# Time mixing: the bonus added by VectorE ahead of one centring product, in place of a second centring product

## The chip, the cores and the metric

The kernel runs on one core of one Trainium2 chip. The metric is the time of one execution on the device in microseconds (us); the figure of a kernel is the median of its runs. The kernel before was run three times: 3210.70, 3211.75 and 3214.01 us, median 3211.75 us.

## What is computed

The reference is one RWKV-like layer (time mixing, then channel mixing) followed by two cross attentions and an MLP. Only the end of time mixing matters here. Per batch and head (32 heads of size S = 16, 128 time steps):

```python
def step(s, rkvw):
    r_t, k_t, v_t, w_t = rkvw
    a = k_t[:, :, :, None] * v_t[:, :, None, :]
    out = jnp.einsum('bhk,bhkd->bhd', r_t, u * a + s)
    return (a + w_t[:, :, :, None] * s, out)
...
a4 = att.reshape(b, l, H, S)
m = jnp.mean(a4, axis=-1, keepdims=True)
var = jnp.mean((a4 - m) ** 2, axis=-1, keepdims=True)
att = ((a4 - m) * jax.lax.rsqrt(var + EPS)).reshape(b, l, E) * gn_w + gn_b
x = x + att * g @ Wo.T
```

`out` is a sum of two parts: what the state gives (`r_t` on `s`) and the bonus (`r_t` on `u * a`, which is `v_t` times the head's sum of `u * r_t * k_t`). The group norm then takes off each head's mean. Taking off the mean is linear: it can be done on the two parts one by one and added, or on their sum.

## The kernel before

Time mixing (`time_mix`, the first 890 us of the execution) works on the 16 batches in four quads (`q`) of four batches. A tile is 128 channels (8 heads) by 512 columns (4 batches of 128 time steps), and there are four channel groups (`f` or `g`, 0 to 3).

For each quad `body` first makes the projections, and then runs the recurrence in 32 steps `t`. Group g = t // 8 takes eight steps, and a step serves two of the 16 value positions of each head. In a step:

- TensorE: `spread(t + 2)`, four matmuls (lines 763 and 764) that spread values over a head's channels into two banks of `vb`; then `accumulate(t - 1)`, two fp32 matmuls (line 683) that sum the products of an earlier step into `mx[g % 2]`. An fp32 matmul stands in the trace as two passes.
- ScalarE: writes the initial state into `vb` (line 452), after `spread`.
- VectorE: a product with the keys (line 581), then two scans over time (line 586) with the result in `state`.
- GpSimd: the product of the state and the receptance (line 308).

`spread(T)` waits until VectorE has ended the scans of step T - 2. `accumulate` waits for GpSimd.

The group norm of group f is laid over the steps after it, at places written by hand: at t = 8f + 10 `attended` (ScalarE, line 352) copies the finished sum from `mx[f % 2]` into `h5`, and `centred` (TensorE, lines 689 and 690) multiplies it by the matrix `centre`, and adds the product of `centre` and the bonus, which GpSimd has left in `vv` (line 272). At 8f + 12 come `square` (ScalarE) and `variance` (TensorE, line 699), at 8f + 14 `deviation` (ScalarE, line 364), `inverse` (VectorE, line 549) and `unpacks` (TensorE, line 705), at 8f + 15 `gated` (VectorE, lines 554 and 558, it waits for `unpacks`). `gate` (TensorE, six matmuls at t = 8f + 3 and 8f + 5) and `bonus` (TensorE line 749, ScalarE line 424 at the next step) lie between them. Thus for f = 0 and 1 all of it falls into the recurrence. For f = 2 `attended` and `inverse` do, and `gated` comes after it. All of group 3's comes after it.

Between two quads stands `joint`: the output product (line 710), the end of the group norm of groups 2 and 3, and the start of the next quad: `norm_stats` and `norm_apply` (VectorE, lines 507 to 519; the latter writes `xf`, which the products of steps 28 and 29 also used), `transposes` (TensorE, line 658, it waits for all four tiles of `norm_apply`), `normalised` (ScalarE, line 333), `shift` (VectorE, lines 523 to 532) and `lora` (TensorE, line 664, each waits for its tile of `shift`). After the last quad stands `closing`, with no next quad to start. Each engine executes its own list in order. `joint` of VectorE before is:

```python
norm_stats(q + 1)
gated(q, 2)
v.wait_ge(rs_used, q * STEPS + (STEPS - 2))
norm_apply(q + 1)
v.wait_ge(rs_ready, q * STEPS + STEPS)
v.wait_ge(rs_used, q * STEPS + STEPS)
shift(q + 1)
```

`rs_used` counts the `accumulate`s.

Of the kernel before, what the change touches and what calls it, by code (L numbers as in the profile page):

```python
# [19 lines left out]
ALU = mybir.AluOpType  # L20
ACT = mybir.ActivationFunctionType
# [5 lines left out]
B, L, E = 16, 128, 512  # L27
# [58 lines left out]
def time_mix(nc, io, x2):  # L86
    J = 6
    MIX = [None, 1, 2, 3, 0, 4]
    STEPS = 32
    with ExitStack() as ctx:  # L90
# [18 lines left out]
        centre = sb("centre", [P, P])  # L109
# [67 lines left out]
        def quad3(ap):  # L177
            return ap.rearrange("p (b t) -> p b t", b=4)
# [60 lines left out]
        @block.gpsimd  # L239
        def _(gp):  # L240
            gp.memset(eps[:], EPS).then_inc(ready, 1)
            gp.memset(rest[:], 0.0).then_inc(x2_out, 16)

            def pack(s, m):
                hi, lo = (h5_split[32 * m:32 * m + 32, 0, :], h5_split[32 * m:32 * m + 32, 1, :]) if m < 4 else (
                    h5_split[0:LORA, 2, :], h5_split[0:LORA, 3, :])
                for k, part in enumerate((hi, hi, lo)):
                    gp.dma_start(packed[32 * k:32 * k + 32, s, :], part).then_inc(pack_in[min(s, 1)], 16)

            def lo(q, j, c):  # L250
                gp.wait_ge(hi_ready, q * 16 + (4 * j - 8 + c + 1))
                gp.tensor_tensor(x_lo[:, c, :], xf[:, c, :], x_hi[:, c, :], ALU.subtract).then_inc(split_ready, 1)

            def value_lo(q, c):
                if q == 0 and c == 0:
                    gp.wait_ge(w_ready, 4)
                gp.wait_ge(v_hi_ready, q * 4 + (c + 1))
                gp.tensor_tensor(quad3(v_lo[:, c, :]), vv[:, c, :, 0:L], quad3(v_hi[:, c, :]), ALU.subtract).then_inc(v_split_ready, 1)

            def receptance_key(q, f):  # L260
                gp.wait_ge(f_free, q * 12 + (8 + f + 1))
                if f == 0:
                    gp.wait_ge(decay_full, q * 4 + 4)
                else:
                    gp.wait_ge(bonus_full, q * 4 + f)
                if f >= 2:
                    gp.wait_ge(cent_full, q * 4 + (f - 1))
                gp.tensor_tensor(quad3(h5[:]), quad3(rr[:, f, :]), kk[:, f, :, 1:L + 1], ALU.mult).then_inc(rk_ready, 1)

            def bonus(q, f):  # L270
                gp.wait_ge(bonus_out, q * 4 + (f + 1))
                gp.tensor_tensor(vv[:, f, :, 1:L + 1], quad3(ew[:]), vv[:, f, :, 1:L + 1], ALU.mult).then_inc(bonus_used, 1)

            gp.wait_ge(w_ready, 2)
            gp.memset(wd[:], 0.0).then_inc(ready, 1)
            for q in range(NQ):
                gp.wait_ge(hl_hi, q * 2 + 1)
                gp.tensor_tensor(h5_split[:, 1, :], h5[:], h5_split[:, 0, :], ALU.subtract).then_inc(hl_lo, 1)
                gp.wait_ge(hl_lo, q * 2 + 1)
                for s in range(3):  # L280
                    pack(s, MIX[s + 2])
                gp.wait_ge(hl_hi, q * 2 + 2)
                gp.tensor_tensor(h5_split[0:LORA, 3, :], h4, h5_split[0:LORA, 2, :], ALU.subtract).then_inc(hl_lo, 1)
                gp.wait_ge(hl_lo, q * 2 + 2)
                pack(3, MIX[5])
                for j in range(2, 5):
                    for c in range(3):
                        lo(q, j, c)
                        if j == 4:
                            value_lo(q, c)  # L290
                    if j == 4:
                        value_lo(q, 3)
                    lo(q, j, 3)
                    if q == 0 and j == 2:
                        gp.wait_ge(w_hi_ready, 4)
                        gp.memset(vv[:, :, :, 0:1], 0.0).then_inc(pad_ready, 1)
                gp.wait_ge(mx_full, q * 20 + 20)
                gp.memset(kk[:, :, :, 0:1], 1.0).then_inc(pad_ready, 1)
                for c in range(EC):
                    lo(q, 5, c)  # L300
                gp.wait_ge(split_ready, q * 16 + 16)
                receptance_key(q, 0)
                for t in range(STEPS):
                    if t >= 4:
                        gp.wait_ge(rs_used, q * STEPS + (t - 3))
                    gp.wait_ge(scanned, q * (3 * STEPS) + 3 * (t + 1))
                    g = t // 8
                    gp.tensor_tensor(prod[t % 4], state[t % 2], rr[:, g:g + 1, :].broadcast_to([P, 2, QT]), ALU.mult).then_inc(rs_ready, 1)
                    for f in range(EC):
                        if t == 8 * f - 2:  # L310
                            receptance_key(q, f)
                        if t == 8 * f + 1:
                            bonus(q, f)

        @block.scalar
        def _(act):
# [20 lines left out]
            def hi(q, j, c, first=False):  # L337
# [6 lines left out]
                elif not first:  # L344
                    act.wait_ge(g_full, q * 4)
                act.activation(x_hi[:, c, :], xf[:, c, :], ACT.Copy).then_inc(hi_ready, 1)

            def attended(q, f):
                act.wait_ge(rs_used, q * STEPS + 8 * (f + 1))
                if f < 3:  # L350
                    act.wait_ge(bonus_full, q * 4 + (f + 2))
                act.activation(h5[:], mx[f % 2][:], ACT.Copy).then_inc(att_ready, 1)

            def square(q, f):
                act.wait_ge(cent_full, q * 4 + (f + 1))
# [35 lines left out]
            def body(q, first):  # L391
# [57 lines left out]
                for t in range(STEPS):  # L449
                    act.wait_ge(vb_full, q * STEPS + (t + 1))  # L450
                    d = 2 * (t % 8)
                    act.activation(vb[:, 2 * (t % 2):2 * (t % 2) + 2, 0:QT:L], s0[:, t // 8, d:d + 2, :], ACT.Copy).then_inc(s0_set, 1)  # L452
                    for f in range(EC):
                        if t == 8 * f + 1:
                            bonus(f)
                        if t == 8 * f + 7:
                            gate(f)
                        if t == 8 * f + 10:
                            attended(q, f)
                        if t == 8 * f + 12:  # L460
                            square(q, f)
                        if t == 8 * f + 14:
                            deviation(q, f)

            def joint(q):
                roots(q + 1)
                attended(q, 3)
                act.wait_ge(rs_ready, q * STEPS + STEPS)
                for c in range(EC):
                    normalised(q + 1, c)  # L470
                square(q, 3)
                deviation(q, 3)
                front(q + 1, False)

            def closing(q):
                attended(q, 3)
                square(q, 3)
                deviation(q, 3)

# [16 lines left out]
        def _(v):  # L496
# [38 lines left out]
            def mix(q, j):  # L535
                for c in range(EC):
# [7 lines left out]
                    v.wait_ge(mx_scaled, q * 20 + (n + 1))  # L544
                    v.tensor_tensor(quad3(xf[:, c, :]), quad3(mx[n % 2][:]), xn[:, c, :, 1:L + 1], ALU.add).then_inc(xf_ready, 1)

            def inverse(q, f):
                v.wait_ge(gstd_ready, q * 4 + (f + 1))
                v.reciprocal(grs[:], grs[:]).then_inc(grstd_ready, 1)
# [17 lines left out]
            def body(q, first):  # L567
# [6 lines left out]
                for t in range(STEPS):  # L574
# [10 lines left out]
                    for d in range(2):  # L585
                        v.tensor_tensor_scan(state[t % 2][:, d, :], wd[:, g].rearrange("p b t -> p (b t)"), pair[:, d, :], 0.0,  # L586
                                             ALU.mult, ALU.add).then_inc(scanned, 1)
                    for f in range(3):
                        if t == 8 * f + 14:
                            inverse(q, f)  # L590
                        if t == 8 * f + 15 and f < 2:
                            gated(q, f)

            def joint(q):
                norm_stats(q + 1)
                gated(q, 2)
                v.wait_ge(rs_used, q * STEPS + (STEPS - 2))
                norm_apply(q + 1)
                v.wait_ge(rs_ready, q * STEPS + STEPS)
                v.wait_ge(rs_used, q * STEPS + STEPS)  # L600
                shift(q + 1)
                inverse(q, 3)
                gated(q, 3)
                mix(q + 1, 1)
                mix(q + 1, 2)
                residual(q)

            def closing(q):
                gated(q, 2)
                inverse(q, 3)  # L610
                gated(q, 3)
                residual(q)
# [25 lines left out]
        def _(pe):  # L638
# [46 lines left out]

            def centred(q, f):
                pe.wait_ge(att_ready, q * 4 + (f + 1))
                pe.wait_ge(bonus_used, q * 4 + (f + 1))
                pe.matmul(mx[f % 2][:], centre[:], h5[:], start=True, stop=False)
                pe.matmul(mx[f % 2][:], centre[:], vv[:, f, :, 1:L + 1], start=False, stop=True).then_inc(cent_full, 1)  # L690

            def variance(q, f):
                if f < 3:
# [1403 lines left out]
```

## Time and profile before

| | |
|---|---|
| median of three runs | 3211.75 us |
| the profiled execution | 3213.54 us |
| its span, as the trace has it | 3211.7 us |
| TensorE busy | 3041.9 us, 95% |
| VectorE busy | 1812.5 us, 56% |
| ScalarE busy | 1195.8 us, 37% |
| GpSimd busy | 571.4 us, 18% |
| mean granted TensorE clock | 0.977 of full speed |

The 1.8 us between the span and the execution's time lie around the program. The busy shares are means over stages that differ a lot. The change touches time mixing alone, where GpSimd is busy too and VectorE is much busier than in the rest, so the shares of the whole say little on it. The stretches of the recurrence are about 108 to 238, 320 to 446, 530 to 654 and 740 to 868 us; the three joints follow the first three, the closing the last.

### The profile page before, as it was taken

What the parts mean: (1) busy time and instruction counts of PE and PEld (TensorE: products, weight loads), DVE (VectorE), ACT (ScalarE), POOL (GpSimd) and SP (SyncE); (2) the same over time, 40 slices, a digit from 0 to 9 for tenths busy, and PEclk for the clock granted to TensorE, in tenths of its full rate; (3) what the DMA queues carried; (4) which work ended last, traced back from release to release, by engine and by line L of the source; (5) the groups of instructions that cost most, each with busy time, mean ns of one, the idle gap of its engine ahead of it and who ended that gap; (6) DMA issues with size and microseconds to landing.
All of it is one profiled execution on the core that took longest, in us unless ns stands there. A gap on an engine that the chain in (4) does not pass through costs nothing.

```text
span 3211.7 us, 41965 instructions
## 1 busy us (share of the span) xinstructions
PE 3041.9 (95%) x15168; PEld 2387.6 (74%) x15168; DVE 1812.5 (56%) x2654; ACT 1195.8 (37%) x2584; POOL 571.4 (18%) x391
## 2 busy tenths in 40 slices
PE   6889899898969799999999999999999999999899
PEld 3545446455457688888888887878888888888787
DVE  5785986868767444445544446455444454444644
ACT  3224123232244343433443434334343454343432
POOL 2664655646500100000100001000000010000100
PEclk8999999999989899999999999999999999999999
DMA  4001000010032411111111111121111111111011
GB/s 131 17 10 38 7 17 31 7 41 1 0 117 82 163 53 36 52 36 53 37 38 51 40 48 35 64 73 46 52 36 52 36 53 36 52 36 42 27 46 59
DMA packets 54178, 148.64 MB, mean 46 GB/s; under 512 B 5936, under 2 KB 7472, under 8 KB 52848
## 3 DMA queue, kind: packets, MB, share of 16 engines
q1 hardware_dynamic: 51792, 144.45, 13.1%
q0 software_dynamic: 2304, 3.15, 0.5%
q8 instruction: 46, 0.75, 0.1%
q14 instruction: 36, 0.29, 0.0%
HBM read 131.85 MB, written 12.58 MB: 45 GB/s over the span
## 4 chain that ended last, share of the span: by engine, by line
PE 64%; DVE 2%; ACT 1%; issue 0%; DMA 0%; ACTq 0%; DVEq 0%
PE ca_ps L60 18%; PE ca_ps L62 18%; PE ca_ps L61 18%; PE ca_ps L1874 4%; PE ca_ps L1858 4%; PE ca_ps L1866 2%; PE ca_ps L1900 0%; DVE ca_stats L68 0%; DVE ca_xres L1635 0%; DMA ca_xres<-in_ctxT 0%; DVE ca_wq_lo L1593 0%; ACT ca_sk L1551 0%; DVE ca_ctx_lo L1666 0%; DVE ca_h_lo L1660 0%; ACT L1551 0%
## 5 line engine op out<-in xcount | busy, mean ns | idle before, releaser
L1635 DVE TENSOR_TENSOR ca_xres<-ca_xres,ca_ps 128x512 f32<-128x512 f32 x384 | 264.1, 688 | 243.9 <-PE ca_ps L62 238.9
L1422 ACT ACTIVATE ca_pr<-ca_ps,ca_nb 128x129 f32<-128x129 f32 x512 | 181.8, 368 | 511.9 <-DVE ca_nb L1618 511.9
L60 PE MATMUL ca_ps<-ca_h_hi,ca_wq_hi 128*128 128x512 f32 x768 | 313.3, 408 | 3.8 <-DVE ca_h_lo L1660 3.3
L586 DVE TENSOR_TENSOR_SCAN tm_xn<-tm_wd,tm_vb 128x512 f32<-128x512 f32 x256 | 298.5, 1208 | 8.9 <-DVE tm_vb L581 0.5
L62 PE MATMUL ca_ps<-ca_h_hi,ca_wq_lo 128*128 128x512 f32 x768 | 302.9, 394 | 0.0
L61 PE MATMUL ca_ps<-ca_h_lo,ca_wq_hi 128*128 128x512 f32 x768 | 301.0, 392 | 0.0
L60 PE MATMUL ca_ps<-ca_wv_hi,ca_ctx_hi 128*128 128x256 f32 x1024 | 297.9, 291 | 0.0
L62 PE MATMUL ca_ps<-ca_wv_hi,ca_ctx_lo 128*128 128x256 f32 x1024 | 287.5, 281 | 0.0
L61 PE MATMUL ca_ps<-ca_wv_lo,ca_ctx_hi 128*128 128x256 f32 x1024 | 287.2, 280 | 0.0
L1375 POOL TENSOR_TENSOR ca_dv<-ca_bvr 128x256 f32<-128x256 f32 x32 | 23.9, 748 | 1452.9 <-DVE ca_v L1603 1443.6
L60 PE MATMUL ca_ps<-ca_wo_hi,ca_ct_hi 128*128 128x512 f32 x640 | 253.5, 396 | 0.2 <-DVE ca_xres L1635 0.2
L61 PE MATMUL ca_ps<-ca_wo_lo,ca_ct_hi 128*128 128x512 f32 x640 | 252.7, 395 | 0.0
L62 PE MATMUL ca_ps<-ca_wo_hi,ca_ct_lo 128*128 128x512 f32 x640 | 252.5, 394 | 0.0
L60 PE MATMUL ca_ps<-ca_ctx_hi,ca_wk_hi 128*128 128x512 f32 x512 | 203.5, 397 | 22.0 <-DVE ca_wk_lo L1598 17.8
L62 PE MATMUL ca_ps<-ca_ctx_hi,ca_wk_lo 128*128 128x512 f32 x512 | 202.8, 396 | 0.0
L61 PE MATMUL ca_ps<-ca_ctx_lo,ca_wk_hi 128*128 128x512 f32 x512 | 201.3, 393 | 0.0
L61 PEld LDWEIGHTS ca_ps<-ca_wv_lo,ca_ctx_hi 128*128 128x128 f32 x1024 | 194.6, 190 | 0.0
L62 PEld LDWEIGHTS ca_ps<-ca_wv_hi,ca_ctx_lo 128*128 128x128 f32 x1024 | 194.2, 190 | 0.0
L60 PEld LDWEIGHTS ca_ps<-ca_wv_hi,ca_ctx_hi 128*128 128x128 f32 x1024 | 192.7, 188 | 0.0
L581 DVE TENSOR_TENSOR tm_vb<-tm_vb,tm_kk 128x1024 f32<-128x1024 f32 x128 | 155.2, 1213 | 45.5 <-ACT tm_vb L452 45.5
L763 PE MATMUL tm_vb<-tm_v_hi,tm_spread_v 128*128 128x512 f32 x256 | 119.5, 467 | 63.7 <-DVE tm_xn L586 63.4
L62 PEld LDWEIGHTS ca_ps<-ca_h_hi,ca_wq_lo 128*128 128x128 f32 x768 | 144.9, 189 | 33.4
(239 smaller groups left out, 6483.1 us busy)
## 6 DMA issues: line engine op xcount, KB each, us to landing
ca_sq<-in_wq SPq DMA_DIRECT2D x49, 512.0 KB, 4.7
ca_so<-in_wo SPq DMA_DIRECT2D x48, 512.0 KB, 3.5
ca_sk<-in_wk SPq DMA_DIRECT2D x33, 512.0 KB, 5.7
ca_sv<-in_wv SPq DMA_DIRECT2D x32, 512.0 KB, 3.5
ca_bvr<-in_bvb SPq DMA_DIRECT2D x32, 256.0 KB, 3.8
tm_xq<-in_x SPq DMA_DIRECT2D x16, 256.0 KB, 2.6
tm_xres<-in_x SPq DMA_DIRECT2D x4, 1024.0 KB, 5.2
x_dram<-tm_xres SPq DMA_DIRECT2D x4, 1024.0 KB, 4.6
```

What stands on the lines that cost most here:

```text
L60: pe.matmul(out, lhs[0], rhs[0], start=first, stop=False)
L61: pe.matmul(out, lhs[0], rhs[1], start=False, stop=False)
L62: return pe.matmul(out, lhs[1], rhs[0], start=False, stop=last)
L581: v.tensor_tensor(pair4, pair4, kk[:, g:g + 1, :, 0:L].broadcast_to([P, 2, 4, L]), ALU.mult).then_inc(scanned, 1)
L586: v.tensor_tensor_scan(state[t % 2][:, d, :], wd[:, g].rearrange("p b t -> p (b t)"), pair[:, d, :], 0.0, ALU.mult, ALU.add).then_inc(scan ...
L763: pe.matmul(vb[:, 2 * (t % 2) + e, :], spread_v[:, d, :], v_hi[:, g, :], start=True, stop=False)
L1375: gp.tensor_tensor(dv[:], bvr[:, 0, :], bvr[:, 1, :], ALU.subtract).then_inc(dv_ready, 1)
L1422: ins = act.activation(pr[hd][:, b, :], ps[:, BANK_SC + b // 2, o:o + KW], ACT.Exp, bias=nbs[hd][:, b:b + 1], scale=SCALE, accum_out=sms[h ...
L1635: v.tensor_tensor(xres[U.h][:, U.quad * 4 + b, :], xres[U.h][:, U.quad * 4 + b, :], ps[:, BANK_O + b % 2, :], ALU.add).then_inc(o_out, 1)
L1858: ins = pe.matmul(ps[:, BANK_SC + b // 2, o:o + KW], qT[hd][:, b * L:(b + 1) * L], kT[hd][:, b, :], start=True, stop=True)
L1866: ins = pe.transpose(ps[:, BANK_TR, b * L:(b + 1) * L], pr[hd][:, b, 0:L], ident[:])
L1874: ins = pe.matmul(ps[:, BANK_PV, b * L:(b + 1) * L], vT[A.quad][:, b, hd * P:(hd + 1) * P], pT[hd][:, b * L:(b + 1) * L], start=True, stop ...
```

## The change

`attended` moves from ScalarE to VectorE. It no longer copies the sum from `mx` into `h5`: it adds the sum to the bonus in place, in `vv`. `centred` multiplies `vv` once, in place of two products that are added. In the recurrence `attended` stands behind the two scans of step 8f + 10 (f = 0, 1, 2). For group 3 it stands in VectorE's `joint` between `gated(q, 2)` and `norm_apply`, where it waits for all 32 `accumulate`s of the quad, and in `closing` behind `gated(q, 2)`. With `h5` no longer used by it, GpSimd's wait for `cent_full` ahead of `receptance_key` goes.

```diff
@@ gpsimd, receptance_key
-                if f >= 2:
-                    gp.wait_ge(cent_full, q * 4 + (f - 1))
@@ scalar
-            def attended(q, f):
-                act.wait_ge(rs_used, q * STEPS + 8 * (f + 1))
-                if f < 3:
-                    act.wait_ge(bonus_full, q * 4 + (f + 2))
-                act.activation(h5[:], mx[f % 2][:], ACT.Copy).then_inc(att_ready, 1)
@@ scalar, body, joint and closing
-                        if t == 8 * f + 10:
-                            attended(q, f)
...
-                attended(q, 3)
@@ vector
+            def attended(q, f):
+                v.wait_ge(rs_used, q * STEPS + 8 * (f + 1))
+                v.wait_ge(bonus_used, q * 4 + (f + 1))
+                v.tensor_tensor(vv[:, f, :, 1:L + 1], quad3(mx[f % 2][:]), vv[:, f, :, 1:L + 1], ALU.add).then_inc(att_ready, 1)
@@ vector, body
                     for f in range(3):
+                        if t == 8 * f + 10:
+                            attended(q, f)
                         if t == 8 * f + 14:
                             inverse(q, f)
@@ vector, joint
                 gated(q, 2)
-                v.wait_ge(rs_used, q * STEPS + (STEPS - 2))
+                attended(q, 3)
                 norm_apply(q + 1)
@@ vector, closing
                 gated(q, 2)
+                attended(q, 3)
                 inverse(q, 3)
@@ tensor, centred
                 pe.wait_ge(att_ready, q * 4 + (f + 1))
-                pe.wait_ge(bonus_used, q * 4 + (f + 1))
-                pe.matmul(mx[f % 2][:], centre[:], h5[:], start=True, stop=False)
-                pe.matmul(mx[f % 2][:], centre[:], vv[:, f, :, 1:L + 1], start=False, stop=True).then_inc(cent_full, 1)
+                pe.matmul(mx[f % 2][:], centre[:], vv[:, f, :, 1:L + 1], start=True, stop=True).then_inc(cent_full, 1)
```

## Rows read from the trace of the kernel before

**Rows 1.** Windows: from:to length, busy us of each engine, granted clock, DMA share, GB/s.
```profile
345.00:446.00 101.00, 90.08 (x303) 50.70 (x302) 92.55 (x84) 22.68 (x50) 66.77 (x32) 0.98 0.03 9
446.00:530.00 84.00, 82.13 (x284) 46.79 (x282) 46.47 (x74) 33.24 (x57) 36.06 (x37) 1.00 0.13 36
```

**Rows 2.** Timeline of VectorE, quad 1: start, length, operation, idle before and its releaser.
```profile
356.35 1.23 DVE L581 TENSOR_TENSOR tm_vb<-tm_vb,tm_kk 128x1024 f32<-128x1024 f32 x1 [1.07 <-ACT tm_vb L452]
...
359.87 1.21 DVE L581 TENSOR_TENSOR tm_vb<-tm_vb,tm_kk 128x1024 f32<-128x1024 f32 x1
...
363.36 1.21 DVE L581 TENSOR_TENSOR tm_vb<-tm_vb,tm_kk 128x1024 f32<-128x1024 f32 x1
...
379.56 0.70 DVE L554 TENSOR_TENSOR tm_pj<-tm_vv,tm_pj 128x512 f32<-128x512 f32 x1 [1.31 <-PE tm_pj L705]
```

**Rows 3.** Timeline of TensorE over the same steps of quad 1.
```profile
360.01 0.50 PE L763 MATMUL tm_vb<-tm_v_hi,tm_spread_v 128*128 128x512 f32 x1 [1.75 <-DVE tm_xn L586]
...
362.76 1.02 PE L689 MATMUL tm_mx<-tm_h,tm_centre 128*128 128x512 f32 x2
363.62 1.02 PE L690 MATMUL tm_mx<-tm_vv,tm_centre 128*128 128x512 f32 x2
...
364.71 0.39 PE L764 MATMUL tm_vb<-tm_v_lo,tm_spread_v 128*128 128x512 f32 x1
...
378.38 1.05 PE L705 MATMUL tm_pj<-tm_grs,tm_unpack 128*128 128x128 f32 x8
```

**Rows 4.** Groups by line, 0 to 1010 us: count, busy us, mean ns, idle before.
```profile
L545 DVE TENSOR_TENSOR tm_xf<-tm_mx,tm_xn 128x512 f32<-128x512 f32 x80 | 55.3, 692 | 2.8
...
L352 ACT ACTIVATE tm_h<-tm_mx 128x512 f32<-128x512 f32 x16 | 9.5, 592 | 20.7 <-PE tm_mx L683 20.7
```

**Rows 5.** Timeline of VectorE, quad 0, `gated` of group 0, then group 1.
```profile
169.45 0.70 DVE L554 TENSOR_TENSOR tm_pj<-tm_vv,tm_pj 128x512 f32<-128x512 f32 x1 [0.88 <-PE tm_pj L705]
...
192.21 1.23 DVE L581 TENSOR_TENSOR tm_vb<-tm_vb,tm_kk 128x1024 f32<-128x1024 f32 x1 [0.58 <-ACT tm_vb L452]
...
205.73 0.69 DVE L554 TENSOR_TENSOR tm_pj<-tm_vv,tm_pj 128x512 f32<-128x512 f32 x1 [1.21 <-PE tm_pj L705]
```

**Rows 6.** A fall of the clock: timelines of TensorE and VectorE, then the window's row.
```profile
417.36 0.50 PE L763 MATMUL tm_vb<-tm_v_hi,tm_spread_v 128*128 128x512 f32 x1 [2.53 <-DVE tm_xn L586]
...
418.60 3.35 PE L683 MATMUL tm_mx<-tm_sx,tm_pick_k 128*128 128x512 f32 x4
...
423.54 1.23 DVE L581 TENSOR_TENSOR tm_vb<-tm_vb,tm_kk 128x1024 f32<-128x1024 f32 x1 [2.75 <-ACT tm_vb L452]
...
417.50:421.50 4.00, 4.00 (x8) 2.20 (x9) 3.26 (x3) 0.00 (x0) 2.88 (x2) 0.58 0.00 0
```

**Rows 7.** Timeline of VectorE in the joint behind quad 1.
```profile
449.51 0.17 DVE L516 RECIPROCAL tm_rstd<-tm_std 128x4 f32<-128x4 f32 x1
449.71 1.92 DVE L519 TENSOR_SCALAR tm_xf<-tm_xq,tm_mv,tm_rstd 128x512 f32<-128x512 f32 x4
452.79 0.18 DVE L523 COPY tm_xn<-tm_prev 128x16 f32 x1 [1.16 <-PE tm_mx L683]
...
458.29 0.75 DVE L532 SCALAR_TENSOR_TENSOR tm_xf<-tm_sx,tm_vec,tm_xn 128x512 f32<-128x512 f32 x1
```

**Rows 8.** Timeline of TensorE in that joint, to its first idle time.
```profile
450.69 1.88 PE L683 MATMUL tm_mx<-tm_sx,tm_pick_k 128*128 128x512 f32 x4
...
453.26 0.60 PE L658 MATMUL tm_mx<-tm_ident,tm_xf 128*128 128x128 f32 x4
...
459.12 4.13 PE L664 MATMUL tm_pj<-tm_xf,tm_lora 128*128 128x512 f32 x8
...
490.44 0.50 PE L653 MATMUL tm_mx<-tm_packed,tm_lora2p 96*128 96x512 f32 x1 [0.69 <-DVE tm_xf L545]
```

**Rows 9.** Timeline of TensorE in the closing.
```profile
876.67 1.02 PE L690 MATMUL tm_mx<-tm_vv,tm_centre 128*128 128x512 f32 x2
...
879.34 0.43 PE L699 MATMUL tm_mx<-tm_ew,tm_head_mean 128*32 128x128 f32 x8
```

More of the change, by code:

```diff
@@ L475, in closing @@
             def closing(q):
-                attended(q, 3)
                 square(q, 3)
```

## The prediction

> **What bounds the kernel now.** The page's busy shares, read first, are means over stages, and most of the span belongs to stages that the change doesn't touch. So I asked for the stretches of time mixing by themselves [rows 1]. In the recurrence (345 to 446 us) VectorE is busy for 92.6 of 101 us and TensorE for 90.1: two engines, both near full. In the joint (446 to 530 us) TensorE is busy for 82.1 of 84 us and VectorE for 46.5: TensorE sets the pace. The change takes work off TensorE and lays work on VectorE, so each stage has to be judged by who waits for whom, in the timelines.
>
> In the recurrence VectorE runs steps of 3.49 us (359.87 to 363.36, [rows 2]) without a pause, but for two waits in each group of eight steps: 1.07 us at step 8f + 10, for ScalarE, and 1.31 us ahead of `gated`, for TensorE's `unpacks` [rows 2]. TensorE starts `spread(8f + 12)` when VectorE's scans release it (idle 1.75 us, [rows 3]) and then has no pause until `unpacks` at 378.38 [rows 3]: gates, variance and both centring products make it fall behind, and VectorE waits for it once. So the bound changes hands: VectorE, then from step 8f + 12 TensorE, until `gated`.
>
> **The change part by part.** *Price of the pieces.* The new VectorE operation is a 128x512 tensor-tensor of one PSUM and one SBUF operand into SBUF. 80 operations of the same form are in the trace at 692 ns [rows 4]. Back to back an operation of VectorE starts a few hundredths before the last one's end, so I take 0.67 us of the queue. That GpSimd works beside it has no price that I can see: the key product, also one PSUM and one SBUF operand, lies beside GpSimd's product in every step and keeps 1.21 us [rows 2]. I allow 0.6 to 0.75 us. On TensorE each `centred` loses one fp32 product: 363.62 - 362.76 = 0.86 us [rows 3]. ScalarE loses 16 copies of 0.59 us [rows 4]; it is busy for 22.7 of 101 us there [rows 1], and the copy lies ahead of no late work, so I take zero.
>
> *Groups 0 and 1, all four quads, no fall of the clock.* `attended` delays every step of VectorE behind 8f + 10 by 0.67 us. The scans of step 8f + 11 then end at 363.36 + 0.67 = 364.03, and `spread(8f + 13)` starts 0.14 us later (the distance from 359.87 to 360.01, [rows 2, 3]), at 364.17; its second matmul follows after 0.34, at 364.51. Before it stood at 364.71 [rows 3]. So of the 0.86 us that TensorE saves, all but about 0.2 us is lost again, since it now waits for VectorE. From there to `unpacks` it stays the later one. `unpacks` and `gated` come 0.2 us earlier. VectorE reaches `gated` 0.67 us later than before, but it had been 1.31 us early: the delay goes into that idle time, which shrinks to about 0.45. Result: -0.19 us for each group in quads 1 and 2. In quads 0 and 3 the idle time is 0.88 us [rows 5], which still holds the 0.67; the steps are a little slower there and I take -0.12. Six such groups: 4 x -0.19 + 2 x -0.12 = -1.0 us. If the idle time weren't there, the group would cost +0.67.
>
> *Groups 1 of quads 0 and 3.* Here the clock fell around `centred`, TensorE is late by more, and VectorE waits 0.58 us ahead of one step and 1.21 ahead of `gated` [rows 5] (quad 3 shows the same pattern). There TensorE's 0.86 us count in full: -0.86 each, -1.7 together, bounds 0 and -1.7, since a fall of the clock needn't come at the same place again.
>
> *Group 2 and the joint, three times.* `attended(q, 2)` delays the end of the scans by 0.67 us, but `gated(q, 2)` comes behind `norm_stats` with no wait, and TensorE arrives at the last `accumulate` by its own pace, 0.19 us earlier: 450.69 - 0.19 = 450.50 [rows 8]. GpSimd's last product, behind scans that end 0.67 us later, is still ready before that. Now the wait that the change adds: `attended(q, 3)` needs the last `accumulate`. VectorE saw it at 452.79 in the trace [rows 7], so about 452.6 now. Behind `attended` on VectorE are queued `norm_apply`, `shift` and all of the next quad. In the trace the small reciprocal of `norm_apply` started at 449.51 and the fourth tile was written at 451.63 [rows 7], 2.12 us in all; TensorE needed it at 453.26 [rows 8], 1.6 us later. Now: 452.6 + 0.67 + 2.12 = 455.4, plus 0.14, is 455.5 for the first transpose: +2.2 us. Does TensorE win it back? `centred(q, 3)` is 0.86 shorter and stands behind the transposes, but `lora` waits for `shift`. The third tile of `shift` was ready at 458.29 + 0.75 = 459.04, and TensorE took it at 459.12 [rows 7, 8]. That was already on time to a tenth, so with `shift` 2.2 us later `lora` is 2.2 us later, and the 0.86 go into the wait. From 459 to 490 TensorE has no idle time [rows 8]: nothing swallows the delay. 3 x 2.2 = +6.6 us; bounds 1.3 (if `lora` had 0.86 of slack) and 2.4 each.
>
> *Closing.* There `norm_apply` is absent. TensorE comes to `centred(3)` 3.4 us after the last `accumulate`, so `attended` is ready. The second product is gone (0.86), and the 0.19 us of group 2 counts: `square`, `variance`, `inverse`, `unpacks` follow one another, from 876.67 to 879.34 [rows 9] and on, all -1.05 us. The removed wait of GpSimd's `receptance_key` is for an event four steps old at that place: zero.
>
> *Sum.* -1.0 - 1.7 + 6.6 - 1.05 = +2.85 us. Against the profiled execution (span 3211.7, with 1.8 us around it 3213.54): 3216.4. That execution lies 1.8 us above the median of the three runs, 3211.75, against which the result will be held: 3214.6. I round to 3215.
>
> **The rivals.** *A, the clock falls in the joint (slower).* What the trace shows: after an idle time of 2.53 us TensorE started again at full clock, and 1 us later four passes took 3.35 us in place of 1.88; the granted clock over 417.5 to 421.5 is 0.58, mostly at the 1.2 GHz level, and VectorE's next wait was 2.75 in place of 1.07, so 1.7 us lost [rows 6, 2]. There are eight idle times of 2.5 us in the recurrences and the clock fell behind four of them; of the twelve of about 1.8 us, behind two. The joint has none in the trace: its granted clock is 1.00 [rows 1]. The change puts one of 2.2 us into each joint, where TensorE is the bound and a fall costs its whole 1.7 us. If it comes in all three: 3214.6 + 5.1 = 3219.7, slower by 0.25%; from two of three it is 3218. By those counts a joint's chance lies between one in six and one in two. The Trainium skill (TensorE: Matmul & The Clock Gate, Part 1: The HAM clock gate) says that the throttled state is the default and that sustained activity releases it; by that rule every new idle time of TensorE speaks against the change, and all three falls, the 3219.7, would be the forecast. The trace agrees that a fall needs an idle time, but not that each brings one.
>
> *B, VectorE sets all of the recurrence (slower).* The idle time ahead of `gated` isn't there to take the 0.67 us, because the wait is put off and not shortened: eight groups at +0.67 in place of -0.34 on average, +8.1 more: 3222.7. Against it: the 1.31 or 0.88 us stand in all eight groups, with the releaser TensorE. It would take a TensorE that `spread` delays by as much again.
>
> *C, the joint costs nothing (faster).* If the transposes weren't behind `norm_apply` for long, or `lora` had slack, each joint would gain its 0.86 us: -2.7 - 1.05 - 2.6 = -6.3, 3205.4. Against it speak the tenth of a microsecond between `shift` and `lora` and the order of VectorE's queue. If TensorE bounded everything, it would be 16 x 0.86 = -13.8 us; the pause-free VectorE steps exclude it.
>
> **How the numbers follow.** Something that one execution can tell from no change is about 0.2% here, 6.4 us. The forecast (+1 to +6 us): 0.65. A: 0.15, of which two thirds over 0.2%. B: 0.08. C: 0.06, of which half over 0.2%. The rest (0.06) is the unknown of where the falls of the clock land in the recurrences, six of them at 1.7 us each, to either side. Slower by over 0.2%: 0.10 + 0.08 + 0.03 = 0.21. Faster: 0.03 + 0.01 = 0.04. Within 0.2%: 0.75. Low end: the joint at its lower bound, 3 x 1.3, gives 3214.6 - 2.7 = 3211.9, and two falls fewer 3208.5. High end: 3219.7 of A plus the 1.7 us that the disturbed groups may not give: 3221.4. Range 3208.5 to 3221.5.
>
> **What would show it.** Right, if in the profile after: TensorE idles about 2.2 us ahead of L658 in each joint, with VectorE as the releaser; ahead of `gated` in quads 1 and 2 VectorE idles about 0.45 us; a TensorE idle of about half a microsecond stands behind the single centring product; `attended` is 0.69 us; the distance from the first scan of a quad to `gated(q, 1)` is 0.2 to 0.4 us shorter. Wrong, if the transposes start without idle time; if VectorE's steps between 8f + 10 and `gated` are longer than 3.49 us; or if `attended` takes over 0.75 us beside GpSimd. The sum fails above all if the falls of the clock change in number: each is worth 60% of the net result.

## The result, and the profile after

The changed kernel takes 3217.54 us (median of 11 runs, 3211.19 to 3219.28), the kernel before on the same chips 3208.94 us (11 runs, 3203.53 to 3214.01). The ratio is 1.0025, with a 95% interval of 1.0016 to 1.0033: slower by 8 us (5 to 11). The forecast was +2.85 us. In absolute terms 3215 was forecast and 3217.54 measured. That looks closer than it is, and by luck: the three runs of the kernel before that the forecast was laid on lie 2.8 us above its median of eleven.

In the profile after, VectorE's timeline of the steps of rows 2 (line 538 is the new `attended`, 574 the key product, 547 `gated`):

```profile
360.77 0.67 DVE L538 TENSOR_TENSOR tm_vv<-tm_mx,tm_vv 128x512 f32<-128x512 f32 x1
361.36 1.22 DVE L574 TENSOR_TENSOR tm_vb<-tm_vb,tm_kk 128x1024 f32<-128x1024 f32 x1
...
364.86 1.21 DVE L574 TENSOR_TENSOR tm_vb<-tm_vb,tm_kk 128x1024 f32<-128x1024 f32 x1
...
380.19 0.70 DVE L547 TENSOR_TENSOR tm_pj<-tm_vv,tm_pj 128x512 f32<-128x512 f32 x1 [0.44 <-PE tm_pj L699]
```

TensorE's timeline over the same steps, which answers to rows 3:

```profile
360.91 0.50 PE L757 MATMUL tm_vb<-tm_v_hi,tm_spread_v 128*128 128x512 f32 x1 [1.75 <-DVE tm_xn L579]
...
365.00 0.50 PE L757 MATMUL tm_vb<-tm_v_hi,tm_spread_v 128*128 128x512 f32 x1 [0.31 <-DVE tm_xn L579]
...
369.13 0.39 PE L757 MATMUL tm_vb<-tm_v_hi,tm_spread_v 128*128 128x512 f32 x1
...
379.01 1.05 PE L699 MATMUL tm_pj<-tm_grs,tm_unpack 128*128 128x128 f32 x8
```

The row of the kernel before that answers to 369.13:

```profile
368.50 0.39 PE L763 MATMUL tm_vb<-tm_v_hi,tm_spread_v 128*128 128x512 f32 x1
```

`attended` costs VectorE's queue 0.59 us (360.77 to 361.36). TensorE now idles 0.31 us behind the single product, because VectorE's scans end later: the next `spread` starts 0.14 us behind them, at 365.00. From `spread(8f + 12)` to `unpacks` it is 379.01 - 360.91 = 18.10 us, where rows 3 give 378.38 - 360.01 = 18.37: 0.27 less, and all of it lies ahead of `spread(8f + 14)` (8.22 against 8.49). VectorE's idle time ahead of `gated` went from 1.31 (rows 2) to 0.44.

The joint behind quad 1, VectorE and then TensorE, which answer to rows 7 and 8 (line 504 and 507 are `norm_apply`, 654 the transposes, 660 `lora`, 649 the last two mixing products ahead of the next quad's projections):

```profile
454.36 0.69 DVE L538 TENSOR_TENSOR tm_vv<-tm_mx,tm_vv 128x512 f32<-128x512 f32 x1 [2.23 <-PE tm_mx L679]
454.97 0.17 DVE L504 RECIPROCAL tm_rstd<-tm_std 128x4 f32<-128x4 f32 x1
455.17 1.91 DVE L507 TENSOR_SCALAR tm_xf<-tm_xq,tm_mv,tm_rstd 128x512 f32<-128x512 f32 x4
```

```profile
452.35 1.88 PE L679 MATMUL tm_mx<-tm_sx,tm_pick_k 128*128 128x512 f32 x4
...
457.14 0.66 PE L654 MATMUL tm_mx<-tm_ident,tm_xf 128*128 128x128 f32 x4 [2.05 <-DVE tm_xf L507]
...
461.64 1.13 PE L660 MATMUL tm_pj<-tm_xf,tm_lora 128*128 128x512 f32 x2 [0.26 <-DVE tm_xf L520]
...
488.85 1.03 PE L649 MATMUL tm_mx<-tm_packed,tm_lora2p 96*128 96x512 f32 x2
```

VectorE stands 2.23 us for the last `accumulate`, and then TensorE stands 2.05 us for `norm_apply`. From the last `accumulate` to the last mixing products it is 488.85 - 452.35 = 36.50 us. The same row of the kernel before starts at 484.93:

```profile
484.93 1.03 PE L653 MATMUL tm_mx<-tm_packed,tm_lora2p 96*128 96x512 f32 x2
```

Against 450.69 (rows 8) that is 34.24 us: the joint is 2.26 us longer. Up to the first `spread` of the next quad, after and then before, a part is won back:

```profile
530.47 0.39 PE L757 MATMUL tm_vb<-tm_v_hi,tm_spread_v 128*128 128x512 f32 x1
```

```profile
526.77 0.39 PE L763 MATMUL tm_vb<-tm_v_hi,tm_spread_v 128*128 128x512 f32 x1
```

From the last `accumulate` that is 78.12 us against 76.08, 2.0 more behind quad 1; behind quads 0 and 2 it is 2.25 more. In the closing the way from the last `accumulate` (875.99) to the last output products (888.90) is 12.91 us; before it was 13.76 (870.66 to 884.42).

So by distances between rows of the profiles: three joints +6.5 us. In quads 1 and 2 each of groups 0, 1 and 2 is 0.27 us shorter, in quads 0 and 3 mostly 0.19, 2.6 together in the four recurrences where the clock doesn't fall. The closing gives -0.85. That is +3.1 us, and five of the eight measured are not in it. The granted clock has most of them. A window in quads 1 and 2 each of the profile before, behind the first idle time:

```profile
375.00:440.00 65.00, 56.45 (x191) 32.07 (x191) 57.93 (x53) 12.40 (x30) 41.63 (x20) 0.97 0.02 5
583.00:650.00 67.00, 58.44 (x197) 33.42 (x196) 60.08 (x55) 13.80 (x33) 42.71 (x20) 0.97 0.03 8
```

and of the profile after:

```profile
375.00:440.00 65.00, 55.80 (x177) 31.55 (x175) 58.12 (x54) 11.45 (x27) 40.30 (x19) 0.95 0.02 8
583.00:650.00 67.00, 57.81 (x190) 32.91 (x189) 60.13 (x56) 12.36 (x29) 41.72 (x20) 0.95 0.03 8
```

A mean of 0.97 is one stretch at the lower level (1.2 GHz), a mean of 0.95 two. Over the four recurrences, behind their first group of steps, the profile before has six such falls and the profile after nine.

### The profile page after: what moved, and what is told of

It reads as the page before. It is cut to its first block, busy times and chain, and to the rows that moved or that the text cites. A ratio compares the mean times of both kernels' runs of the same rounds, so it can differ in the third digit from the quotient of the medians.

```text
span 3215.7 us, 41878 instructions
## 1 busy us (share of the span) xinstructions
PE 3033.6 (94%) x15136; PEld 2380.1 (74%) x15136; DVE 1821.9 (57%) x2670; ACT 1189.3 (37%) x2568; POOL 568.8 (18%) x391
## 4 chain that ended last, share of the span: by engine, by line
PE 64%; DVE 2%; ACT 1%; issue 0%; DMA 0%; DVEq 0%; ACTq 0%
PE ca_ps L60 18%; PE ca_ps L62 18%; PE ca_ps L61 18%; PE ca_ps L1868 4%; PE ca_ps L1852 4%; PE ca_ps L1860 2%; PE ca_ps L1894 1%; DVE ca_stats L68 0%; DVE ca_xres L1629 0%; DVE ca_ctx_lo L1660 0%; DMA ca_xres<-in_ctxT 0%; DVE ca_wq_lo L1587 0%; ACT ca_sk L1545 0%; DVE ca_h_lo L1654 0%; ACT L1545 0%
```

## The experiments

The kernel before ran beside each; the interval is the 95% one of the ratio to it. A difference in us is that of the ratio, and can be 2 to 3 us off the difference of the two medians (e6: -9.9 and -7.7).

### Does the joint's wait cost, and does the addition's place?

**e1_joint_order**

```diff
                 gated(q, 2)
-                attended(q, 3)
+                v.wait_ge(rs_used, q * STEPS + (STEPS - 2))
                 norm_apply(q + 1)
+                attended(q, 3)
```

> The changed kernel, but in VectorE's joint the old wait and norm_apply stand ahead of attended(q, 3) again. Theory J (the joint's new wait is the main cost, 2.2 us each of three): the transposes start with no idle time again, 6.6 us less than the changed kernel, so about +1.4 us on the kernel before (ratio 1.0004) if the clock falls as often as in the changed kernel's profile, and -4 us (0.9988) if it falls as often as before. Rival N (the joint's wait is hidden or paid back later): no more than 2 us less than the changed kernel, +6 us on before (1.0019).

Measured: 3203.07 us, ratio 0.9989 (0.9980 to 0.9998), -3.5 us. That is 11.5 us less than the changed kernel, of which the three joints explain 6.5; its profile has two to three falls of the clock fewer in the recurrences, too. VectorE and then TensorE in its joint:

```profile
445.66 1.91 DVE L507 TENSOR_SCALAR tm_xf<-tm_xq,tm_mv,tm_rstd 128x512 f32<-128x512 f32 x4
447.79 0.69 DVE L538 TENSOR_TENSOR tm_vv<-tm_mx,tm_vv 128x512 f32<-128x512 f32 x1 [0.22 <-PE tm_mx L680]
```

```profile
445.79 1.88 PE L680 MATMUL tm_mx<-tm_sx,tm_pick_k 128*128 128x512 f32 x4
...
448.36 0.60 PE L655 MATMUL tm_mx<-tm_ident,tm_xf 128*128 128x128 f32 x4
...
480.01 1.03 PE L650 MATMUL tm_mx<-tm_packed,tm_lora2p 96*128 96x512 f32 x2
```

The transposes have no idle time ahead of them, `attended` lies in a wait that VectorE had anyway, and the joint is 480.01 - 445.79 = 34.22 us, as before. Theory J holds, rival N falls. It also shows that the product saved ahead of `lora` is worth nothing there: 34.22 against 34.24.

**e2_add_at_9**

```diff
                     for f in range(3):
-                        if t == 8 * f + 10:
+                        if t == 8 * f + 9:
                             attended(q, f)
```

> The changed kernel with attended one step earlier, behind the scans of step 8f + 9, where VectorE would wait 1.07 us for ScalarE anyway. Theory H (the saved product of 0.86 us was lost because TensorE then waits for the delayed scans): the addition costs VectorE nothing, the idle time of 0.3 us of TensorE behind centred goes, VectorE's idle time ahead of gated is 0.45 us again but for the other reason, and each of twelve groups ends 0.6 us earlier: 7 us less than the changed kernel, about +1 us on before (1.0003). Rival V (VectorE's queue pays the 0.6 us wherever the addition stands): no change to the changed kernel, +8 us on before (1.0025).

Measured: 3206.72 us, ratio 0.9996 (0.9987 to 1.0005), no difference to before and 9 us less than the changed kernel. VectorE and TensorE in group 0 of quad 1:

```profile
350.89 0.67 DVE L538 TENSOR_TENSOR tm_vv<-tm_mx,tm_vv 128x512 f32<-128x512 f32 x1
352.04 1.23 DVE L574 TENSOR_TENSOR tm_vb<-tm_vb,tm_kk 128x1024 f32<-128x1024 f32 x1 [0.49 <-ACT tm_vb L444]
...
374.39 0.70 DVE L547 TENSOR_TENSOR tm_pj<-tm_vv,tm_pj 128x512 f32<-128x512 f32 x1 [0.45 <-PE tm_pj L699]
```

```profile
355.70 0.50 PE L757 MATMUL tm_vb<-tm_v_hi,tm_spread_v 128*128 128x512 f32 x1 [1.75 <-DVE tm_xn L579]
...
358.44 1.02 PE L684 MATMUL tm_mx<-tm_vv,tm_centre 128*128 128x512 f32 x2
359.19 0.51 PE L757 MATMUL tm_vb<-tm_v_hi,tm_spread_v 128*128 128x512 f32 x1
```

The addition sits in the old wait for ScalarE (1.07 us in rows 2, now 0.49 behind it), TensorE goes from the product to `spread` with no idle time, and from `spread(8f + 12)` to `gated` it is 374.39 - 355.70 = 18.69 us, where before has 19.55 (rows 2 and 3) and the changed kernel 19.28. That is the whole 0.86 us of the product. Theory H holds. In this profile the clock fell in all three joints (in one profile of the changed kernel it fell in two, in its others in none). The window at the one behind quad 1:

```profile
449.50:456.50 7.00, 6.24 (x26) 3.60 (x28) 4.89 (x10) 3.96 (x6) 0.00 (x0) 0.76 0.00 0
```

The joint is then 482.61 - 445.48 = 37.13 us, 0.63 more than the 36.50 without a fall. Up to the next quad's first `spread` the five falls in joints of e2 and of the changed kernel cost 0.6 to 1.1 us each. So +6.5 and 1.1 + 0.6 + 0.7 us lie in e2's joints, which is why it comes out level with before and not faster.

**e3_both** has both edits.

> Both edits: attended at 8f + 9, and norm_apply ahead of attended(q, 3). If J and H both hold, the product's 0.86 us count 8 times in the recurrences, 3 times ahead of the joints and about twice in the closing: 11 us less than before (0.9965) with the clock falls of before, 6 us less (0.998) with those of the changed kernel. If only J holds: -4 to +1 us. If neither: +8 us.

Measured: 3199.89 us, ratio 0.9980 (0.9971 to 0.9989), -6.4 us. Both theories hold here too; the gain is at the lower end of what was expected, with seven falls in its recurrences.

### Is it the product, or the wait?

**e4_product_twice**

```diff
+                pe.matmul(mx[f % 2][:], centre[:], vv[:, f, :, 1:L + 1], start=True, stop=True)
                 pe.matmul(mx[f % 2][:], centre[:], vv[:, f, :, 1:L + 1], start=True, stop=True).then_inc(cent_full, 1)
```

> The changed kernel with the centring product done twice over the same input (the second overwrites the first), so TensorE has the work of before and VectorE the addition. Without the clock each group costs 0.3 us more than in the changed kernel (12 groups, and 0.86 in the closing: +4.5 us). Theory F (TensorE's lighter load in the recurrence makes its clock fall more often, nine times in the profile where it was six): the falls go back to about six, which gives 5 us back, so the time is that of the changed kernel within 2 us (+8 us on before, 1.0025). Rival R (the number of falls is chance and has nothing to do with the product): the falls stay at eight or nine on average and the time is 4 to 5 us over the changed kernel (+13 us, 1.004).

Measured: 3218.81 us (5 runs), ratio 1.0042 (1.0028 to 1.0055), +13.5 us. The time is that of rival R. The profile speaks the other way: it has four falls in the recurrences. But the profiled execution took 3212.9 us, 6 us under the kernel's median, so it is not a typical one, and the run decides nothing between F and R. What it shows of the steps is clean:

```profile
376.22 0.70 DVE L547 TENSOR_TENSOR tm_pj<-tm_vv,tm_pj 128x512 f32<-128x512 f32 x1 [0.72 <-PE tm_pj L700]
```

With TensorE's old load VectorE still idles 0.72 us ahead of `gated`: 1.31 less the 0.59 of the addition. So the addition at step 8f + 10 costs nothing by itself; that idle time takes it.

**e5_wait_alone** is the kernel before with

```diff
                 gated(q, 2)
-                v.wait_ge(rs_used, q * STEPS + (STEPS - 2))
+                v.wait_ge(rs_used, q * STEPS + STEPS)
                 norm_apply(q + 1)
```

> The kernel before with one edit: norm_apply in VectorE's joint waits for all 32 accumulates of the quad instead of 30, with no addition on VectorE. Theory J: norm_apply starts at 452.79 in the numbers of rows 7 and ends 2.12 us later, so the first transpose comes 1.8 us later than before, three times, +5.4 us (ratio 1.0017). Rival N (that delay is hidden): no change.

Measured: 3217.96 us (8 runs), ratio 1.0029 (1.0018 to 1.0040), +9.3 us, more than expected. VectorE and TensorE in its joint:

```profile
450.26 0.18 DVE L516 RECIPROCAL tm_rstd<-tm_std 128x4 f32<-128x4 f32 x1 [3.01 <-PE tm_mx L683]
```

```profile
448.34 1.88 PE L683 MATMUL tm_mx<-tm_sx,tm_pick_k 128*128 128x512 f32 x4
...
452.45 0.66 PE L658 MATMUL tm_mx<-tm_ident,tm_xf 128*128 128x128 f32 x4 [1.36 <-DVE tm_xf L519]
...
484.17 1.03 PE L653 MATMUL tm_mx<-tm_packed,tm_lora2p 96*128 96x512 f32 x2
```

484.17 - 448.34 = 35.83 us, 1.59 more than before; up to the next `spread` the three joints give +4.6 us. The other 4.7 us are an excess like that of the changed kernel, in a kernel with no addition on VectorE and both products on TensorE. Its profile has eight falls in the recurrences, which behind their first groups take 4.7 us more than on average in the profiles of before.

### What do the falls of the clock cost?

The kernels e6, e7 and e8 have useless matmuls in TensorE's idle times of the recurrence:

```diff
+            def filler(q, gates, n):
+                pe.wait_ge(g_ready, q * 4 + gates)
+                for i in range(n):
+                    pe.matmul(pj[1][:], spread_v[:, 0, :], x_hi[:, 0, :], start=True, stop=True)
...
+                    if t % 8 == 7 and 8 < t < 31:
+                        filler(q, t // 8 + 1, 8)
+                    if t % 8 == 1 and t > 8:
+                        filler(q, t // 8, 5)
```

**e6_before_filled**

> The kernel before with useless matmuls in TensorE's idle times of the recurrence (eight of 0.23 us each ahead of the 2.53 us wait at steps 8f + 16, five ahead of the 1.75 us wait at steps 8f + 10); their result is overwritten, the output is the same. Theory C (the idle time is what lets the clock fall there, and each of six falls costs 1.7 us): no fall between the first and the last group of a recurrence, 10 us less than before (0.9969). Rival R (the falls come by something else, or cost nothing): no change.

Measured: 3200.03 us (6 runs), ratio 0.9969 (0.9957 to 0.9981), -9.9 us: as theory C has it. One filled idle time and two windows:

```profile
409.14 2.40 PE L695 MATMUL tm_pj<-tm_x_hi,tm_spread_v 128*128 128x512 f32 x8
412.24 0.50 PE L768 MATMUL tm_vb<-tm_v_hi,tm_spread_v 128*128 128x512 f32 x1 [0.69 <-DVE tm_xn L586]
```

```profile
375.00:440.00 65.00, 62.43 (x218) 36.42 (x217) 60.88 (x57) 14.96 (x32) 41.03 (x20) 1.00 0.03 9
583.00:650.00 67.00, 64.42 (x223) 37.28 (x222) 62.80 (x65) 15.09 (x32) 41.55 (x19) 1.00 0.03 8
```

The idle time of 2.53 us is 0.69, the granted clock is 1.00 in both windows, and no fall is left behind the first group of any of the four recurrences. 9.9 us (6 to 14) for the four to six falls that the kernel before has is 1.7 to 2.5 us each. The distances between rows give 1.65: behind the first group the four recurrences of this profile take 356.6 us, and those of before with six falls 366.5.

**e7_after_filled** is the changed kernel with it.

> The changed kernel with the same useless matmuls. It is to be compared with the filled kernel before: with no falls in either what is left is the work by the steps of the prediction. Theory S (joints +6.8, groups -2, closing -0.9 us, as the distances in the profiles have it): 4 us more than the filled kernel before, so about -6 us on the kernel before (0.998). Theory X (the change costs 8 us by something that is neither a step of the prediction nor a fall of the clock): 8 us more than the filled kernel before.

Measured: 3205.28 us, ratio 0.9987 (0.9978 to 0.9996), -4.2 us. Against the filled kernel before it is 0.9987 / 0.9969 = 1.0018, or 5.3 us by the medians (3205.28 - 3200.03 is of the same chip's runs). Expected were 4 by theory S and 8 by theory X. It lies nearer to S, but with two intervals of 0.001 to each side the times of this pair don't exclude X. The pair's two profiles, neither with a fall behind a first group, show the change's steps alone: joints +6.6 us, recurrences behind the first group -2.7, which are the distances found above. In these stages theory X has nothing to explain. The filling took 12 us off the changed kernel and 10 off the kernel before.

**e8_both_filled** is e3 with the filling.

> attended at 8f + 9 and norm_apply ahead of attended(q, 3), with the useless matmuls. Theories S and C: 10.6 us less than the filled kernel before, and 20 us less than before (0.9937). If the falls aren't removed by filling: 0.998, as without it.

Measured: 3190.44 us (5 runs), ratio 0.9938 (0.9924 to 0.9951), -20 us, as expected. This is the fastest version of the study, under both kernels.

### Are there more falls because of the change?

These four are the kernel before and the changed kernel with no edit, for a second and third profile of each.

**e9_before_again**

> The kernel before, unchanged, for a second profile: how many times the clock falls behind the idle times of the recurrences in another execution. Theory F (the change itself makes falls more frequent): six, give or take one, as in the first profile. Rival P (the number changes from one execution to the next, whatever the kernel): anywhere from three to nine.

**e10_after_again**

> The changed kernel, unchanged, for a second profile. Theory F: eight to ten falls in the recurrences, as in the first profile. Rival P: three to nine.

**e11_before_third**

> The kernel before once more. Theory F: five to seven falls in the recurrences. Rival P: a number unlike that of the other two profiles.

**e12_after_third**

> The changed kernel once more. Theory F: eight to ten falls in the recurrences. Rival P: a number unlike that of the other two profiles, with the executions' times in the order of their numbers, 1.7 us for each.

Measured, with the first profiles and those of the other kernels beside them; the falls are counted in the record of the granted clock, behind the first group of steps of each recurrence:

| kernel | time of the profiled execution | falls in the recurrences |
|---|---|---|
| before | 3213.54, 3205.64, 3208.45 us | 6, 4, 6 |
| after | 3217.54, 3215.98, 3217.91 us | 9, 8, 8 |
| e1, e3 (no late `norm_apply`) | 3200.59, 3198.56 us | 6, 7 |
| e5, e2, e4 (late `norm_apply`) | 3217.03, 3205.84, 3212.94 us | 8, 6, 4 |

The window of quad 2 in the third profile of before, and then of after, as one row each of this count:

```profile
583.00:650.00 67.00, 58.44 (x200) 33.41 (x200) 60.38 (x55) 14.96 (x32) 41.38 (x20) 0.97 0.03 8
```

```profile
583.00:650.00 67.00, 57.83 (x190) 32.91 (x189) 60.23 (x56) 12.67 (x29) 41.58 (x21) 0.95 0.02 8
```

Three more falls on average in the changed kernel (25 against 16 in three profiles each), and no overlap: theory F's numbers, though three profiles are few. The means of the three spans of each, by stage:

| stage (of a profile) | before | after | difference |
|---|---|---|---|
| up to the first `spread` | 106.2 us | 104.7 us | -1.5 |
| four recurrences, to the last `accumulate` | 534.1 | 536.0 | +1.9 |
| the three stretches from there to the next quad's first `spread` | 226.8 | 233.9 | +7.1 |
| behind the last `accumulate` of quad 3 | 2340.4 | 2340.6 | +0.3 |
| span | 3207.4 | 3215.3 | +7.9 |

In the recurrences +1.9 us is -2.6 by the steps, +3.9 by the falls behind the first groups (8.7 us for 5.3 falls before, 12.6 for 8.3 after, so 1.6 and 1.5 each) and +0.7 in the first groups. The +7.1 are the joints' 6.5 and two falls in joints.

Why there are more falls is another matter. The reason that theory F gives, TensorE's lighter load, doesn't fit: e1 and e3 have the single product and six and seven falls, e5 has both products and eight. What the kernels with many falls share is the late `norm_apply`, in six profiles of four kernels 9, 8, 8, 8, 6 and 4 against 6, 4, 6, 6 and 7 without it: a leaning and not proof. Counted by place, it is weaker still. Behind the 2.53 us idle time of group 1 in quads 1 and 2 (66 us behind the quad's first `spread`) the clock fell in one of six cases in the profiles of before and in six of six in those of the changed kernel, more than half of the surplus; but it also fell there in four of four in e1 and e3, without the late `norm_apply`. How a delay elsewhere would reach that idle time no run here shows. It stays open.

## Why the prediction was right or wrong

**The bound of each stage: right.** In the recurrence the bound changes hands inside each group, and the idle time ahead of `gated` took the addition: 1.31 to 0.44 (0.45 forecast), and 0.72 in e4 with the addition alone.

**Price of the addition: 0.67 forecast, 0.59 measured** as distance in the queue, 0.67 as its length, beside GpSimd's product or not. It makes the group -0.27 us in place of -0.19. The idle time behind the product was put at about half a microsecond; it is 0.31.

**The lost 0.86 us: right.** TensorE's idle time behind the product is there (0.31 us), and e2, which takes away only the delay of the scans, gets the rest of the 0.86 back.

**The joint: right, 2.2 forecast, 2.0 to 2.26 measured**, with TensorE's idle time of 2.05 us and VectorE as its releaser, and `lora` on `shift`'s heels. e1 takes it away completely, and e5 gives 1.59 of it without any of the rest. The match has a little luck in it: the forecast's 2.2 already holds the 0.19 us that group 2 wins, so from the last `accumulate` on it said 2.4. And "nothing swallows the delay" is not quite so: behind quad 1, 0.2 us go into the idle time at the end of rows 8 (0.69, 0.46 after).

**The closing: -1.05 forecast.** The stretch behind the last `accumulate` is 0.85 shorter; the rest is group 2's share ahead of it.

**The disturbed groups: wrong, and with them the clock's share of the sum.** The -1.7 us rested on two falls that would come at the same places again. The effect itself exists: where the clock fell just ahead of `centred`, the way from one `spread` to the next is 5.77 us before (184.56 to 190.33) and 4.91 in the changed kernel's third profile (817.57 to 822.48), 0.86 less. But it is no saving to count on, as the places changed from profile to profile (two, none and one such falls before; two, two and one after). The step that was off is the number of falls. The text took six as given and named a change of their number only as what would upset the sum. There were eight to nine against four to six, and that made +3.9 us where the sum has nothing.

**The sum: near for the steps by luck, low for the whole.** The steps without the falls measure +6.5 - 2.6 - 0.85 = +3.1 us, close to +2.85. But without the credit of 1.7 (and with the two groups at their undisturbed -0.12) the forecast's own steps give 6.6 - 1.05 - 4 x 0.19 - 4 x 0.12 = +4.3: it had the joints 0.7 too dear and the groups 0.6 too small a gain, and the credit stood in for both. To the 3.1 of the steps come 3.9 us by the falls of the recurrences, 0.7 in their first groups and 0.6 in the joints, less 0.3 in the stages around: the 7.9 of the table, to a tenth. The forecast's single number lies outside the measured 5 to 11. That the kernel would come out slower by over 0.2% had a chance of 0.21; it is 0.25%.

**Rival A: wrong in place and size.** It foresaw that the clock would matter, but in the joints. There it fell twice in the nine joints of three profiles of the changed kernel and in all joints of e2, and cost 0.6 to 1.1 us and not 1.7. Behind the transposes TensorE waits for `shift` anyway (0.26 us ahead of `lora`, gone where the clock falls), and the slower matmuls go into that wait; in e4, with both products and so no such wait, a fall in a joint cost 1.4 us. Where about 1.6 us are paid is the recurrence: e6 shows it. The Trainium skill (TensorE: Matmul & The Clock Gate, Part 1: The HAM clock gate) says that the throttled state is the default and that activity releases it; by that rule idle time is what speaks for a fall. The traces agree for the idle times of the recurrences, where filling them ended the falls (granted clock 1.00), but not for the joint, where seven of nine joints of the changed kernel show none behind 2.05 us.

**Rivals B and C: fell**, B by the 0.44 us ahead of `gated`, C by the joints that are 2.0 to 2.26 us longer.

## What to carry to other kernels

An operation laid on a second engine was free where that engine waited anyway, and the place is a matter of one step: the same addition cost 0.6 of TensorE's saved 0.86 us behind step 8f + 10 and nothing behind 8f + 9, where VectorE waited for ScalarE. Look at what is queued behind a new wait on the engine: it was `norm_apply` behind the addition that cost 2.0 to 2.3 us each time, and two lines in the other order brought it back. And where TensorE has idle times of a few microseconds, count the falls of its clock in several profiles before a sum to a microsecond is trusted; a few matmuls into the idle time, with their result thrown away, show what the falls cost.

## What was not expected of the hardware

Useless work made the kernel faster: eight matmuls of 0.23 us in idle times of 2.53 us, and five in those of 1.75 us, took 9.9 us off the kernel before (interval 6 to 14), and 12 and 13 us off the changed kernel and e3 (by their ratios, from runs beside different runs of before). The number of falls in the recurrences differs between executions of one kernel (4 to 6, 8 to 9), and the stages around differ too: up to the first recurrence's start the profiles differ by 4.5 us (first `spread` at 102.5 to 107.0 us), with code that no edit touched. That is more than the whole of the change's steps, 3.1 us.
